# Attention: VectorE in place of ScalarE copies the turned maxima out of PSUM

## The reference

```python
qkv = (x @ W_qkv + b_qkv).reshape(B, S, 3, H, hd)
q, k, v = (qkv[:, :, 0], qkv[:, :, 1], qkv[:, :, 2])
attn = jnp.einsum('bqhd,bkhd->bhqk', q, k) / jnp.sqrt(jnp.asarray(hd, x.dtype))
attn = jax.nn.softmax(attn, axis=-1)
attn_out = jnp.einsum('bhqk,bkhd->bqhd', attn, v).reshape(B, S, D)
...
moe_out = jnp.einsum('bsef,bse->bsf', expert_out, combine)
return attn_out + moe_out
...
x = _layernorm(x + _L0_ffn_ref(x, ...), axis=-1)
```

## Time and profile before

| | before |
|---|---|
| median of 3 runs | 3752.07 us (3751.63 to 3758.32) |
| profiled execution | 3751.49 us |
| span in its profile | 3749.7 us |
| mean granted TensorE clock | 0.973 |
| busy share PE / DVE / ACT / POOL | 93 / 87 / 69 / 48% |

### The profile page before, as it was taken

One profiled execution on the slowest core, in us unless ns is written; L12 is line 12 of the kernel. 1 busy time (PEld: TensorE's weight loads), 2 busy tenths in 40 slices (PEclk: granted clock), 3 DMA queues, 4 the chain that ended last, 5 costly groups with the idle time before them and its releaser, 6 DMA issues.

```text
span 3749.7 us, 119956 instructions
## 1 busy us (share of the span) xinstructions
PE 3492.4 (93%) x52122; PEld 1583.7 (42%) x52122; DVE 3251.9 (87%) x3105; ACT 2589.8 (69%) x3896; POOL 1785.5 (48%) x1565
## 2 busy tenths in 40 slices
PE   5999999999999989998599999999999999999997
PEld 3655555454555545555332423324233242332422
DVE  5899989989999998998589797997979979799796
ACT  3665757666575766655269497695976959769598
POOL 4787878878887887888031210312103121031210
PEclk7999999999999999999799999999999999999999
DMA  3443545444453444444340602406024060240600
GB/s 95 132 121 105 149 109 137 115 132 124 109 152 100 136 121 126 125 106 115 91 69 2 102 13 42 73 2 93 22 39 76 2 94 21 39 76 2 91 13 13
DMA packets 145233, 307.78 MB, mean 82 GB/s; under 512 B 24484, under 2 KB 64068, under 8 KB 144452
## 3 DMA queue, kind: packets, MB, share of 16 engines
q1 hardware_dynamic: 144708, 300.10, 35.2%
HBM read 230.68 MB, written 35.13 MB: 71 GB/s over the span
## 4 chain that ended last, share of the span: by engine, by line
PE 22%; ACT 10%; DVE 10%; issue 9%; DMA 0%; SPq 0%; ACTq 0%; DVEq 0%; POOL 0%
ACT probs L1532 10%; PE ps L1332 7%; PE ps L1319 6%; DVE neg_max L1640 3%; PE ps L1367 2%; PE ps L1280 2%; PE ps L1442 2%; PE ps L1347 1%; PE ps L1380 1%; DVE acc L1774 1%; DVE acc L1763 1%; DVE att L1684 1%; DVE x1T L1622 1%; DVE x1T L1620 1%; DVE acc L1766 0%
## 5 line engine op out<-in xcount | busy, mean ns | idle before, releaser
L350 POOL TENSOR_TENSOR z<-z,c_rep 128x1024 f32<-128x1024 f32 x512 | 1412.8, 2770 | 330.9 <-DVE z L867 322.3
L1532 ACT ACTIVATE probs<-ps,e_scale 128x512 f32<-128x512 f32 x2048 | 1242.5, 696 | 118.2 <-PE ps L1319 117.8
L867 DVE TENSOR_TENSOR_SCAN z<-dA,ps 128x1024 f32<-128x1024 f32 x512 | 1157.8, 2278 | 130.2 <-PE ps L408 82.2
L1640 DVE TENSOR_REDUCE neg_max<-ps 128x1 f32<-128x1024 f32 x1024 | 1191.8, 1218 | 58.9 <-PE ps L1280 57.5
L708 ACT ACTIVATE dA<-rep,a_rep 128x1024 f32<-128x1024 f32 x512 | 565.4, 1142 | 217.9 <-DVE z L867 214.4
L408 PEld LDWEIGHTS ps<-diag,u_t 64*64 64x64 f32 x32768 | 531.9, 135 | 389.1 <-issue 388.7
L1319 PE MATMUL ps<-q_st,k_st 50*128 50x512 f16 x2048 | 648.9, 389 | 26.6 <-ACT probs L1532 20.1
L1332 PE MATMUL ps<-probs,v_h 128*32 128x256 f32 x8192 | 657.2, 395 | 0.6 <-ACT o_sb L1539 0.6
L408 PE MATMUL ps<-diag,u_t 64*64 64x64 f32 x32768 | 599.0, 222 | 59.7 <-DVE z L867 40.5
L1280 PE MATMUL ps<-k_st,q_st 48*128 48x512 f16 x2048 | 614.0, 388 | 7.5 <-DVE neg_max L1640 6.6
L427 PE MATMUL ps<-z,eye 128*64 128x512 f32 x2048 | 506.1, 615 | 2.8 <-POOL z L350 2.3
(11 more groups left out here) (189 smaller groups left out, 3107.2 us busy)
## 6 DMA issues: line engine op xcount, KB each, us to landing
c_rep<-c_scratch SPq DMA_DIRECT2D x512, 256.0 KB, 4.0
rep<-delta SPq DMA_DIRECT2D x128, 256.0 KB, 4.5
q_st<-qk_halves SPq DMA_DIRECT2D x192, 128.0 KB, 10.0
k_st<-qk_halves SPq DMA_DIRECT2D x192, 128.0 KB, 10.5
qk_halves<-qk_parts SPq DMA_DIRECT2D x32, 512.0 KB, 10.6
x_nat<-in_x SPq DMA_DIRECT2D x9, 1024.0 KB, 7.9
x_rows<-x_nat SPq DMA_DIRECT2D x9, 1024.0 KB, 6.8
xT<-in_xT SPq DMA_DIRECT2D x8, 1024.0 KB, 7.5
```

The lines of the kernel that those rows point to most:

```text
L350: pool.tensor_tensor(z[:, k % ZR, :], z[:, k % ZR, :], c_rep[:, slot, :], ALU.mult).then_inc(s_zc, 1)
L867: dve.tensor_tensor_scan(z[:, k % ZR, :], dA[:, k % AR, :], pair(1 + k % 2), 0.0, ALU.mult, ALU.add).then_inc(s_z, 1)
L1532: act.activation(probs[:, kt, half * HALF:(half + 1) * HALF], ps[:, ring_bank(("probs", h, 2 * kt + half)), :], ACT.Exp, scale=e_scale[:, ...
L1640: dve.tensor_reduce(neg_max[:, h % 2, qt:qt + 1], pair(qt % 2), AX.X, ALU.max, negate=True).then_inc(s_mx, 1)
```

## The change

ScalarE's `take_max` (the copy of the rows to `m_rows`) is removed at all its places: behind the ninth exponential of each head but the last, and behind u = 25 of the experts for head 0. VectorE gets `take_rows` with the same two waits: behind the fifth maximum (qt = 4) of a step for head h+1; for head 15 behind `take_x` of the next batch; for head 0 behind the maxima of u = 26 in the experts.

```diff
-            def take_max(b, h):
-                g = b * HEADS + h
-                act.wait_ge(s_mt, g + 1)
-                act.wait_ge(s_md, g * 64 + 16)
-                act.activation(m_rows[:, :], ps[0:2 * TT, ring_bank(("rows", h, 0)), 0:P], ACT.Copy).then_inc(s_mr, 1)
...
-                        if turned and kt == 4 and half == 0:
-                            take_max(b, h + 1)
...
-                    if u == 25:
-                        take_max(b, 0)
...
+            def take_rows(b, h):
+
+                g = b * HEADS + h
+                dve.wait_ge(s_mt, g + 1)
+                dve.wait_ge(s_md, g * 64 + 16)
+                dve.tensor_copy(m_rows[:, :], ps[0:2 * TT, ring_bank(("rows", h, 0)), 0:P]).then_inc(s_mr, 1)
...
                     if qt == 0 and not before:
                         join(b, TT - 1)
+                    if qt == 4:
+                        take_rows(b, h + 1)
                     if qt == 6 and before:
                         normalise(b, h - 1)
...
                     take_x(b + 1, 0)
                     take_x(b + 1, 1)
+                take_rows(b, HEADS - 1)
+                if more:
                     split_qk(b + 1, 0)
...
                             for unit in (unit, unit + 1):
                                 take_max(b, unit // TT, unit % TT)
+                            if unit == TT + 5:
+                                take_rows(b, 0)
```

More of the change, by code:

```diff
@@ L1539, in take_o, with step @@
                 act.activation(o_sb[:, :], ps[:, 6, 0:T // QUARTERS], ACT.Copy).then_inc(s_o, 1)
-            def take_max(b, h):
-                g = b * HEADS + h
-                act.wait_ge(s_mt, g + 1)
-                act.wait_ge(s_md, g * 64 + 16)
-                act.activation(m_rows[:, :], ps[0:2 * TT, ring_bank(("rows", h, 0)), 0:P], ACT.Copy).then_inc(s_mr, 1)
-            def step(b, h, before, turned):
+            def step(b, h, before):
                 for kt in range(TT):
@@ L1552, in step @@
                             take_o(b, h - 1)
-                        if turned and kt == 4 and half == 0:
-                            take_max(b, h + 1)
             def heads(b):
[L1557 to L1560, removed]
+                step(b, 0, False)
+                for h in range(1, HEADS):
+                    step(b, h, True)
                 take_o(b, HEADS - 1)
```

## The result

The changed kernel takes 3868.75 us (median of 5 runs, 3863.38 to 3874.84), the kernel before 3751.63 us (5 runs, 3749.89 to 3758.32). The ratio is 1.0308, 95% interval 1.0294 to 1.0323: slower by 3.1%. The profiled execution took 3865.29 us.

The account below looks back on a forecast made before the run. Three engines are nearly full in each head, with the copy gating TensorE's sixth step. Terms 104.0 + 4.9 + 1.6 − 0.2 = 110.3 us on the profiled 3751.49 give 3861.8, forecast 3862; range 3842 to 3886.

Parts of the forecast that it names:

- The bound: Steady heads, period 9.93 us: three engines nearly full; TensorE's sixth step waits for the copy's bank, starting 0.07 us behind it.
- The copy leaves ScalarE: In each head, freeing ScalarE's 0.16 us is worth 0; upper bound 18 us.
- The copy on VectorE: Behind the fifth maximum: start 1.13 us later, copy 0.28, release 0.07; TensorE's sixth step comes 1.00 us later.
- Nothing is given back: From the sixth step on, no present wait is shortened by the stall; the head period becomes 10.94 us.
- rival 1: Waits before the fifth maximum absorb part of the stall; all of both gone gives 3810 us; chance 0.06.
- The count and the small terms: Copies for heads 2 to 14 add 104.0 us, head 1 4.9, head 0 1.6; ScalarE saves 0.2 in the last batch.
- rival 4's small form: Head 0's slow clock stretch reaches twice as far into the next head, some 2 us a batch, 3878; chance 0.04.
- Faster: Copy fits VectorE's 0.30 us idle time and ScalarE's 0.16 comes back in each head: 3734 us; chance 0.03.
- no change: The rows' bank is needed late enough, or VectorE reaches the copy sooner: 3752, up to 3761 us; chance 0.03.
- rival 3: No change: the rows' bank is needed late enough or VectorE copies sooner; 3752, up to 3761 us; chance 0.03.
- Absorption: TensorE's bank wait and VectorE's 0.30 us shrink before the fifth maximum; 3810 us if both vanish; chance 0.06.
- The clock rival: Longer stalls bring TensorE to half clock for two steps in each of 112 heads: about 4028 us; chance 0.05.

Follow-up runs that it names:

- e2_scalar_late: The kernel before, with ScalarE's copy behind the tenth exponential in place of the ninth; 3811.73 us, ratio 1.0151 to the kernel before.
- e8_scalar_twice: The kernel before, with a second ScalarE copy, to an unread tile, behind the ninth exponential; 3778.00 us, ratio 1.0057 to the kernel before.
- e1_fourth: The changed kernel, with VectorE's copy behind the fourth maximum in place of the fifth; 3757.42 us, ratio 1.0003 to the kernel before.
- e5_fourth_twice: The changed kernel, with two VectorE copies, the first to an unread tile, both behind the fourth maximum; 3760.27 us, ratio 1.0007 to the kernel before.
- e4_twice: The changed kernel, with VectorE copying the rows twice behind the fifth maximum, first to an unread tile; 3915.28 us, ratio 1.0426 to the kernel before.
- e3_turn_late: The changed kernel, with the rows turned one step later and their place in the ring moved too; 3802.04 us, ratio 1.0119 to the kernel before.

## Why the prediction was right

*The bound.* Right in what the forecast uses: from its place before, the end of the copy can't move back without TensorE's sixth step moving with it. One exponential later on ScalarE costs 0.57 us a head (`e2_scalar_late`), one copy more on ScalarE 21 us in all (`e8_scalar_twice`). But the earlier trace rows doesn't show that the sixth step was being held, as the prediction reads it. With the copy early (`e1_fourth`) the weight loads are idle for as long, only put down to another cause. The waits of before, 2440 to 2540 (us in total, times, longest), 14.6 us in these three rows, and of `e1_fourth` in the same window, 15.0:

```profile
PEld ps L1319 <- issue: 6.0, 21, 0.4
PEld ps L1319 <- DMA q_st<-m_rows: 4.5, 10, 0.8
PEld ps L1319 <- ACT m_rows L1545: 4.1, 10, 0.4
```

```profile
PEld ps L1319 <- issue: 14.0, 40, 0.4
PEld ps L1319 <- DMA q_st<-m_rows: 0.6, 1, 0.6
PEld ps L1319 <- DVE m_rows L1636: 0.4, 1, 0.4
```

TensorE's matmuls have no idle time before the sixth step in either kernel, and it starts 0.94 us behind the same scoresT in both. So the copy came just in time before: it cost nothing, and had next to nothing to spare.

*The copy leaves ScalarE: 0.* Right. The `e1_fourth` kernel has all of this gain and no measurable time from it.

*The copy on VectorE.* The estimate was 284 ns (its terms give 283), the trace has 0.27 us. The Trainium skill (VectorE: DVE Perf Modes, TRN2 errata) gave 0.258, a little under it. The copy starts 1.15 us behind the maximum instead of 1.13, and the release takes 0.05 us instead of 0.07. The sum of the three, 1.48 forecast, is 1.47 (2512.53 to 2514.00); the small errors cancel.

*Nothing is given back.* Right, and this was the step that decided between forecast and rival 1. All three waits of before keep their length, and the period is 10.93 to 10.94 us (forecast 10.94).

*The count and the small terms.* The steady heads, from the eleventh exponential of head 1 to that of head 13, grew by 12 × 1.00 in each batch, 96.2 us in all by the two traces (96 forecast). From head 0 to head 1 it is 11.9 us in eight batches in place of 8. This is where TensorE comes from half clock, and the slow stretch reaches further in some batches. In the last one the windows show it up to 3678.60, and in the kernel before only between 3571.90 and 3575.10:

```profile
3668.50:3678.60 10.10, 9.48 (x54) 1.75 (x56) 7.24 (x8) 6.57 (x11) 0.00 (x0) 0.50 0.00 0
```

```profile
3571.90:3575.10 3.20, 3.20 (x23) 0.64 (x22) 2.44 (x3) 2.27 (x5) 0.00 (x0) 0.50 0.01 1
```

Of the eight batches this is where the two kernels differ most; over all eight the slow stretches around head 0 sum to 65 us in place of 48. But other kernels vary there too: `e5_fourth_twice`, whose heads keep the period of before, has 58 us of them, and takes 4.1 us more than the kernel before from head 0 to head 1. So the 16 us of rival 4's small form (chance 0.04) didn't come, and whether the 3.9 us above the forecast are a small share of it or chance is not shown.

Up to the eleventh exponential of head 0 it is 5.5 us (4.9 forecast). Between the batches it is 5.4 us in place of 1.6, and the 0.2 that ScalarE was to save in the last batch didn't come. Here the kernels whose VectorE program is that of before lie between 1.4 us less (`e2_scalar_late`) and 6.2 us more (`e8_scalar_twice`), so the 5.4 can't be put down to the copy or cleared of it. The scan and the first experts happened to be 5.2 us shorter. Spans together: +113.8 us against 110.3 forecast; the timed runs give +116 (ratio 1.0308). The 96 us of the steady heads are a forecast that came true; that the total lies so close is in part luck, since the other parts are off by up to 5 us each way.

*The rivals.* Faster and no change would have needed the copy to be done by the sixth step; it is 0.92 us late. Where it is done by then (`e1_fourth`, ratio 1.0003), rival 3's time comes out. Absorption is refuted by the unchanged waits. The clock rival is wrong for this kernel (1.00 in its steady heads), but it was nearer than its chance of 0.05 said: 0.2 us more of a wait brings slow stretches in 13 of 96 heads (`e4_twice`).

## What to carry to other kernels

A small copy between engines is priced by what stands in front of it in its new queue, and by who waits for its end, not by how full the engines are: the same copy cost 1.00 us a head behind one maximum and nothing behind the one before. Look up what the instruction in front of it waits for; here it waited for the step just in front of the one that the copy releases, which makes the three into a serial chain. Then follow each wait of the loop from the stall onward: if the chain that ends it starts behind the stall, the stall is paid in full.

## What was not expected

TensorE's clock made a growing stall dearer than linear here. The second copy adds 24 us by the chain and about 44 in time, the third 24 and about 78 (3915 to 3993); the granted clock in the steady heads goes 1.00, 0.96, 0.93 in the batch that is shown. The wait that TensorE had in each head differs by only 0.2 us from one of these kernels to the next (0.92, 1.12, 1.32), and the slow stretches in the 96 steady heads number 0, 13 and 40. And the margin of the rows' DMAs is thin: in `e3_turn_late` the next head's first step began 3.54 us behind the copy's end, where before it was 3.86, so of these the DMAs need at most 3.54, and the wait of the weight load says that they need about as much.
